# One core's decayed attention: value products dealt over two heads of every four, five probability slots, PSUM banks three and three, and the program's loops written out

## Chip, core and metric

The kernel is one program on 1 core of a Trainium2 chip. It takes the reference's inputs and gives its output. The metric is the device time in microseconds (us), the median of several runs; the profile is one more execution, taken by the hardware profiler.

## What is computed

`x` is 8 sequences of 512 tokens of 128 channels, in float32. Four blocks follow one another, each on a layer norm of `x` and each added to `x`: a Mamba block with a cumulative branch (stage "m" of the kernel), two transformer layers with windowed attention and a gated feed-forward (stage "t0"), the decayed attention below (stage "a"), and the same two layers again (stage "t1").

```python
q, k, v = qkv[0], qkv[1], qkv[2]                 # 16 heads of 8 channels, from x @ Wqkv.T + b
scores = einsum('bhsd,bhtd->bhst', q, k) / sqrt(8)
decay = exp(-abs(distance_decay[0]) * abs(s - t))
attn = softmax(scores * decay, axis=-1)          # 512 x 512 per head
out = einsum('bhst,bhtd->bhsd', attn, v)
return out.transpose(...).reshape(b, s, e) @ out_w.T + out_b
```

## The kernel before

Every engine has an instruction list of its own, written by hand, and the lists meet only through semaphores. Each stage walks over its B = 8 sequences; the first and the last one or two are written out, and the ones between are a hardware loop (`Fori`), whose body is in the program once and ends in a branch back. All semaphore targets in a loop body are computed from the loop's register. Between stages all engines wait for each other (`meet`).

Stage "a", for sequence q and head h (16 heads), with query tiles or key chunks 0 to 3:

- TensorE `score` (line 1165): one bf16 product of 72 by 128 with 72 by 512 makes the scores of one query tile t; it goes to `bank[t % 2]`, so two PSUM banks alternate. It waits until VectorE has read the score two before it.
- VectorE `scale_scores` (1319): times the decay, and the row maximum, PSUM to the tile `S[h % 4, t]`.
- GpSimd `subtract_max` (1403): maximum minus score, in place.
- TensorE `turn` (1174): four 128 by 128 transposes bring key chunk c of the head into `bank[2 + c]`: four banks, one for each chunk. The chunk-0 turn waits for the head's four `subtract_max`, and each turn for the exponentials of four turns earlier.
- ScalarE `exps` (1276): the exponential of the turned chunk, from its bank to `AT[h % 4, c]`.
- TensorE `weigh` (1185): once four heads are done, their probabilities times their values (and ones, for the sums) for key chunk c, four products side by side in `bank[6]`. With c = 0 it waits for the division of the group before.
- ScalarE `copy_oT` (1280), TensorE `untranspose` (1192), VectorE `divide` (1331, 1334): the result of four heads is copied, turned back and divided by its sums.

TensorE's list sets the order. A sequence is 64 steps u = 4h + c. In each it issues `SCORES[u % 16]` scores (they run LEAD = 6 scores ahead of the turns), then perhaps a `weigh`, then the turn. Before the change the four `weigh` of a group stand in the four steps of the next group's first head, with two scores in front of each; the next twelve steps have eight scores. `untranspose` stands behind the second head, and `divide` in VectorE's list behind the first score (t = 0) of a group.

Once for each sequence there are further steps: projections of the next sequence on TensorE (1149, 1154), their copies on ScalarE (1268, 1269), the values' copy `take_values` on VectorE (1325), the split of queries and keys into three bf16 parts on GpSimd (`split`, 1390, 1394, 1397, behind heads 6 and 8), the bias and norm work for the next stage, the output projection of the sequence before, and SyncE's transfers of the parts through DRAM.

Of the kernel before, what the change touches and what calls it, by code (L numbers as in the profile page):

```python
# [21 lines left out]
P = 128  # L22
# [31 lines left out]
LEAD = 6  # L54
SCORES = (2, 2, 2, 2, 1, 1, 1, 0, 1, 1, 0, 1, 0, 1, 0, 1)

# [81 lines left out]
def hybrid_block(nc, a, out):  # L138
# [3 lines left out]
    with ctx:  # L142
# [78 lines left out]
        amax = mem.take(4, TPS)  # L221
        AT = mem.take(4, TPS, L)
        aoT = mem.take(L)
# [99 lines left out]
        MAMBA_LOADS, FOLD_LOADS = 11, 3  # L323
        COMBOS = 2 * PARTS
        HALF = HA // 2 * L
        FIRST = 2 * TPS
# [15 lines left out]
        def hold(eng):  # L342
# [7 lines left out]
                   (hidden_ready, 2), (down_added, 1),  # L350
                   (scaled_done, 2), (aexp_done, TPS), (at_done, 16), (ao_ready, 1), (av_out, TPS),
                   (xt_ready, 1), (lt_ready, 1), (mm_ready, 1), (mixed, 1), (gT_ready, 1), (fuse_added, 1))
# [110 lines left out]
        def transformer_sp(sp, call, meets):  # L463
# [10 lines left out]
            for l in range(DEPTH):  # L474
                q0 = l * B + call * SEQS
                if l:
# [4 lines left out]
                    load_ff(sp, l)  # L481
                with sp.Fori(0, B - 1) as s:
# [25 lines left out]
        def transformer_pe(pe, call, meets):  # L508
# [151 lines left out]
            for l in range(DEPTH):  # L660
# [18 lines left out]
                attention_sequence(q0, False, True)  # L679
                with pe.Fori(1, B - 1) as s:  # L680
                    attention_sequence(q0 + s, True, True)
# [8 lines left out]
                ff_round(q0 + 1, 1, False, True)  # L690
                with pe.Fori(2, B - 2, 2) as s:
                    ff_round(q0 + s, 0, False, True)
                    ff_round(q0 + s + 1, 1, False, True)
# [7 lines left out]
        def transformer_act(act, call, meets):  # L701
# [75 lines left out]
            for l in range(DEPTH):  # L777
# [7 lines left out]
                attention_sequence(q0, False, True)  # L785
                with act.Fori(1, B - 1) as s:
                    attention_sequence(q0 + s, True, True)
# [6 lines left out]
                ff_affine(q0, 0)  # L794
                with act.Fori(0, B - 2, 2) as s:
                    ff_round(q0 + s, 0, True)
                    ff_round(q0 + s + 1, 1, True)
# [33 lines left out]
        def transformer_dve(dve, call, meets):  # L831
# [125 lines left out]
            for l in range(DEPTH):  # L957
# [10 lines left out]
                if l == 0:  # L968
                    with dve.Fori(1, B - 2) as s:
                        attention_sequence(s, q0 + s, True, True, True)  # L970
                    attention_sequence(B - 2, q0 + (B - 2), True, True)
                else:
                    with dve.Fori(1, B - 1) as s:
                        attention_sequence(s, q0 + s, True, True)
# [7 lines left out]
                ff_round(1, q0 + 1, 1, False, True, last_layer)  # L982
                with dve.Fori(2, B - 2, 2) as s:
                    ff_round(s, q0 + s, 0, False, True, last_layer)
                    ff_round(s + 1, q0 + s + 1, 1, False, True, last_layer)
# [14 lines left out]
        def transformer_pool(pool, call, meets):  # L1000
# [58 lines left out]
            for l in range(DEPTH):  # L1059
# [6 lines left out]
                if l == 0:  # L1066
                    with pool.Fori(0, B - 2) as s:
                        attention_sequence(s, q0 + s, True, True)
                    attention_sequence(B - 2, q0 + (B - 2), True)
                else:  # L1070
                    with pool.Fori(0, B - 1) as s:
                        attention_sequence(s, q0 + s, True)
# [3 lines left out]
                meet(pool, l * 2 + meets + 1)  # L1076
                with pool.Fori(0, B - 2, 2) as s:
# [21 lines left out]
        def decayed_sp(sp):  # L1099
# [19 lines left out]
            load_ff(sp, 0)  # L1119
            with sp.Fori(0, B - 1) as q:  # L1120

# [11 lines left out]
        def decayed_pe(pe):  # L1133
# [24 lines left out]
            def score(q, k):  # L1158
                if k == 0:
                    pe.wait_ge(combos_in[0], (q + 1) * (16 * COMBOS))  # L1160
                if k == 32:
                    pe.wait_ge(combos_in[1], (q + 1) * (16 * COMBOS))
                h, t = k // TPS, k % TPS
                pe.wait_ge(scaled_done, 64 * q + k + 1)
                nc.tensor.matmul(bank[t % 2][:, :], QC[0:COMBO, h, t * P:(t + 1) * P], KC[0:COMBO, h, :],  # L1165
                                 start=True, stop=True).then_inc(score_done, 1)

            def turn(q, h, c):
# [4 lines left out]
                for t in range(TPS):  # L1173
                    last = nc.tensor.transpose(bank[2 + c][:, t * P:(t + 1) * P], S[:, h % 4, t, c * P:(c + 1) * P], ident)  # L1174
                last.then_inc(at_done, 1)

            def weigh(q, g, c):

                pe.wait_ge(aexp_done, 64 * q + 16 * g + c + 17)
                if c == 0:  # L1180
# [3 lines left out]
                for i in range(4):  # L1184
                    last = nc.tensor.matmul(bank[6][32 * i:32 * i + 2 * DA, :], AV[:, c, 4 * g + i, :], AT[:, i, c, :],
                                            start=(c == 0), stop=(c == TPS - 1), skip_group_check=True)
# [25 lines left out]
            def sequence(q, before, more):  # L1212
                k = LEAD
                for u in range(HA * TPS):
                    h, c = u // TPS, u % TPS
                    for _ in range(SCORES[u % 16]):
# [4 lines left out]
                        k += 1  # L1221
                    if h % 4 == 0:
                        if h:
                            weigh(q, h // 4 - 1, c)
                        elif before:
                            weigh(q - 1, 3, c)
                    turn(q, h, c)
                    if c < TPS - 1:
                        continue
                    if h == 1:  # L1230
                        if before:
                            untranspose(q - 1, 3)
                        project_v(q)
                    elif h % 4 == 1:
                        if before and h == 5:
                            out_transpose(q - 1, True, more)
                        untranspose(q, h // 4 - 1)
# [13 lines left out]
            sequence(0, False, True)  # L1251
            with pe.Fori(1, B - 1) as q:
                sequence(q, True, True)
# [7 lines left out]
        def decayed_act(act):  # L1261
# [9 lines left out]
            def exps(q, h):  # L1271
                for c in range(TPS):
                    act.wait_ge(at_done, 64 * q + 4 * h + c + 17)
                    if h % 4 == 0:
                        act.wait_ge(av_out, 16 * q + h + c + 1)
                    nc.scalar.activation(AT[:, h % 4, c, :], bank[2 + c][:, :], ACT.Exp, scale=-1.0).then_inc(aexp_done, 1)  # L1276

# [8 lines left out]
            def sequence(q, before, more):  # L1286
                for h in range(HA):
                    exps(q, h)
                    if h == 0 and before:
                        copy_oT(q - 1, 3)  # L1290
                    elif h % 4 == 0 and h:
                        copy_oT(q, h // 4 - 1)
# [12 lines left out]
            sequence(0, False, True)  # L1305
            with act.Fori(1, B - 1) as q:
                sequence(q, True, True)
# [4 lines left out]
        def decayed_dve(dve):  # L1312
            def scale_scores(q, h, t):
                if t == 0:
# [3 lines left out]
                off = (TPS - 1 - t) * P  # L1318
                nc.vector.tensor_tensor_reduce(out=S[:, h % 4, t, :], in0=bank[t % 2][:, :], in1=decay[:, off:off + L],  # L1319
                                               scale=1.0, scalar=-3.0e38, op0=ALU.mult, op1=ALU.max,  # L1320
# [21 lines left out]
            def sequence(q, before, more, norm_more=False, norm_next=False):  # L1342
                for h in range(HA):
                    for t in range(TPS):
                        scale_scores(q, h, t)
                        if t == 0 and h < 8 and h % 4 == 0 and before:
# [18 lines left out]
            sequence(0, False, True, True)  # L1365
            with dve.Fori(1, B - 2) as q:
                sequence(q, True, True, True)
# [6 lines left out]
        def decayed_pool(pool):  # L1374
# [46 lines left out]
            for t in range(2):  # L1421
                for step in range(3):
                    split(0, t, step)
            with pool.Fori(0, B - 2) as q:
                sequence(q, True, True)
# [99 lines left out]
        def mamba_pe(pe):  # L1525
# [124 lines left out]
            sequence(0, 0, False, True, True)  # L1650
            with pe.Fori(0, (B - 4) // 2) as s:
                sequence(2 * s + 1, 1, True, True, True)
# [10 lines left out]
        def mamba_act(act):  # L1663
# [76 lines left out]
            sequence(0, 0, False, True, True)  # L1740
            with act.Fori(0, (B - 4) // 2) as s:
                sequence(2 * s + 1, 1, True, True, True)
# [8 lines left out]
        def mamba_dve(dve):  # L1751
# [118 lines left out]
            sequence(0, 0, False, True, True, True)  # L1870
            with dve.Fori(0, (B - 4) // 2) as s:
                sequence(2 * s + 1, 1, True, True, True, True)
# [9 lines left out]
        def mamba_pool(pool):  # L1882
# [100 lines left out]
            sequence(0, 0, False, True, True, True)  # L1983
            with pool.Fori(0, (B - 4) // 2) as s:
                sequence(2 * s + 1, 1, True, True, True, True)
# [110 lines left out]
```

## Time and profile before

| | us |
|---|---|
| median of 3 runs (2385.03 to 2386.71) | 2386.45 |
| the profiled execution's own time | 2385.01 |
| its span, first to last instruction | 2383.2 |
| stage "m" and start | 0 to 330 |
| stage "t0" | 330 to 1053 |
| stage "a" (first score to last addition) | 1071.9 to 1635.1 |
| stage "t1" | 1635.1 to 2383.2 |

A timeline row gives an instruction's start, its duration, and in brackets how long its engine had been idle and who ended that. TensorE's ends are modelled: a matmul's duration reaches past the start of the next one, so the true cost of a step on TensorE is the distance between starts. An idle time in brackets is therefore shorter than the delay of the start. Times are us from the start of the span.

### The profile page before, as it was taken

To read this page: it belongs to the slowest core of one execution; us is meant where nothing else is said; L and a number is where in the kernel's file an instruction comes from. 1 tells how busy PE (TensorE), PEld (TensorE's weight loads), DVE (VectorE), ACT (ScalarE), POOL (GpSimd) and SP (SyncE) were. 2 spreads that over 40 slices of the span, in tenths; PEclk is the share of its full clock that TensorE was granted. 3 is DMA by queue.
4 is the path that set the end of the run, shared out by engine and by line. 5 is a ranking of instruction groups with operands and counts; after the bars stand their busy time and mean duration, and the time that the engine had idled before them with its cause. 6 is when DMAs were issued, how large, how long until landed. Compare 5 with 4: busy or idle time off the path is not lost. (4 is left out here: it accounts for less than half of the span.)

```text
span 2383.2 us, 60302 instructions
## 1 busy us (share of the span) xinstructions
PE 2184.3 (92%) x19744; PEld 1490.5 (63%) x19760; DVE 1627.2 (68%) x3905; ACT 1489.7 (63%) x4130; POOL 1679.1 (70%) x1712
## 2 busy tenths in 40 slices
PE   6998789998989999859999999998999978999979
PEld 4766557776557777535655656564777755677755
DVE  5777578886557777537666667675878745777755
ACT  3556368887358887325655556554888843888853
POOL 5777788886168888228777777766889822888842
PEclk8999899999999999889999999998999999999999
DMA  4000011111111111112111111101111112111101
GB/s 111 1 0 1 6 27 34 40 37 30 48 36 36 36 34 33 27 58 58 54 42 34 52 53 37 49 21 25 28 34 40 43 23 51 36 34 36 39 21 50
DMA packets 121250, 86.69 MB, mean 36 GB/s; under 512 B 85560, under 2 KB 102160, under 8 KB 118800
## 3 DMA queue, kind: packets, MB, share of 16 engines
q1 hardware_dynamic: 119248, 82.70, 14.3%
q10 hardware_dynamic: 1856, 2.23, 0.3%
q8 instruction: 69, 1.13, 0.2%
q14 instruction: 77, 0.63, 0.1%
HBM read 30.38 MB, written 8.39 MB: 16 GB/s over the span
## 5 line engine op out<-in xcount | busy, mean ns | idle before, releaser
L1319 DVE CUSTOM_DVE_ANT_0 store<-bank,store 128x512 f32<-128x512 f32 x512 | 340.1, 689 | 170.2 <-PE bank L1165 108.6
L1403 POOL TENSOR_SCALAR store<-store 128x512 f32<-128x512 f32 x512 | 349.7, 694 | 149.5 <-DVE store L1319 147.4
L1276 ACT ACTIVATE store<-bank 128x512 f32<-128x512 f32 x512 | 287.1, 603 | 251.2 <-PE bank L1174 247.7
L730 ACT ACTIVATE store<-bank,store 128x128 f32<-128x128 f32 x1024 | 364.2, 378 | 68.5 <-DVE store L860 68.4
L1010 POOL TENSOR_TENSOR store<-store 128x16 f32<-128x16 f32 x128 | 372.5, 2910 | 26.6 <-DVE store L856 26.6
L1004 POOL TENSOR_TENSOR store<-store 128x512 f32<-128x512 f32 x256 | 321.0, 1275 | 85.0 <-DVE store L847 83.7
L1174 PEld LDWEIGHTS bank<-store 128*128 128x128 f32 x2048 | 241.4, 142 | 130.4 <-ACT store L1276 74.1
L1174 PE MATMUL bank<-store 128*128 128x128 f32 x2048 | 298.3, 278 | 0.0
L519 PE MATMUL bank<-store 128*128 128x512 f32 x512 | 270.1, 615 | 7.1 <-DVE store L835 6.6
L1019 POOL TENSOR_TENSOR store<-store 128x512 f32<-128x512 f32 x256 | 261.5, 1043 | 17.4 <-POOL store L1010 11.4
L860 DVE TENSOR_REDUCE store<-bank 128x4 f32<-128x512 f32 x256 | 165.0, 686 | 130.4 <-PE bank L553 130.4
L736 ACT ACTIVATE store<-bank 128x512 f32<-128x512 f32 x256 | 157.8, 616 | 114.0 <-PE bank L566 114.0
L730 ACT ACTIVATION_READ_ACCUMULATOR store<-bank,store 128x1 f32 x1024 | 222.1, 217 | 0.0
L1165 PE MATMUL bank<-store 72*128 72x512 bf16 x512 | 183.2, 389 | 39.5 <-DMA store<-parts 22.0
L638 PE MATMUL bank<-store 128*128 128x512 f32 (+1 forms) x384 | 189.4, 630 | 27.8 <-DVE store L933 22.8
L533 PEld LDWEIGHTS bank<-store 128*128 128x128 f32 x1024 | 116.3, 141 | 129.1 <-POOL store L1019 103.2
L533 PE MATMUL bank<-store 128*128 128x128 f32 x1024 | 154.8, 281 | 35.1 <-POOL store L1019 33.1
L842 DVE TENSOR_TENSOR store<-bank,store 128x512 f32<-128x512 f32 x256 | 174.5, 682 | 12.9 <-issue 6.2
L847 DVE TENSOR_TENSOR store<-bank,store 128x512 f32<-128x512 f32 x256 | 174.4, 681 | 0.0
L592 PEld LDWEIGHTS bank<-store 128*128 128x128 f32 x1024 | 133.5, 192 | 63.8 <-ACT store L741 38.7
L762 ACT ACTIVATE store<-bank,store 128x512 f32<-128x512 f32 (+1 forms) x96 | 65.9, 686 | 170.7 <-PE bank L638 168.4
L566 PEld LDWEIGHTS bank<-store 128*128 128x128 f32 x1024 | 120.8, 141 | 75.9 <-issue 68.1
(199 smaller groups left out, 4457.3 us busy)
## 6 DMA issues: line engine op xcount, KB each, us to landing
store<-store SPq DMA_DIRECT2D x256, 128.0 KB, 2.3
store<-parts SPq DMA_DIRECT2D x96, 192.0 KB
parts<-store SPq DMA_DIRECT2D x16, 384.0 KB, 3.6
store<-store SPq DMA_DIRECT2D x128, 32.0 KB
store<-store SPq DMA_DIRECT2D x128, 31.8 KB
store<-store SPq DMA_DIRECT2D x32, 127.0 KB
store<-in_L_ffn_wqkv_dram SPq DMA_DIRECT2D x4, 768.0 KB, 4.6
out_dram<-store SPq DMA_DIRECT2D x8, 256.0 KB, 2.5
```

Source lines behind the costliest of these rows:

```text
L519: nc.tensor.matmul(bank[i][:, :], hT[:, j * P:(j + 1) * P], wqkv[:, i * INNER:(i + 1) * INNER], start=True, stop=True).then_inc(qk_done, 1)
L533: last = nc.tensor.transpose(bank[5 + i][:, b * P:(b + 1) * P], roped[:, i, b * P:(b + 1) * P], ident)
L638: nc.tensor.matmul(to, w1[:, half * HID + at:half * HID + at + n], fnT[:, odd, :], start=True, stop=True).then_inc(up_done, 1)
L730: last = nc.scalar.activation(prob[:, e, b, :], bank[3 + e][:, b * P:(b + 1) * P], ACT.Exp, bias=nmax[:, e, b:b + 1], accum_out=psums[:, h ...
L1004: nc.gpsimd.tensor_tensor(straight[:, at, :], straight[:, at, :], turned[:, at, :], ALU.add).then_inc(add_done, 1)
L1010: nc.gpsimd.tensor_tensor(flat, flat, minus_half[:, 0:2 * H], ALU.pow).then_inc(norm_done, 1)
L1019: nc.gpsimd.tensor_tensor(roped[:, i, :].rearrange("p (h d) -> p h d", d=DH), straight[:, at, :].rearrange("p (h d) -> p h d", d=DH), bc(n ...
L1165: nc.tensor.matmul(bank[t % 2][:, :], QC[0:COMBO, h, t * P:(t + 1) * P], KC[0:COMBO, h, :], start=True, stop=True).then_inc(score_done, 1)
L1174: last = nc.tensor.transpose(bank[2 + c][:, t * P:(t + 1) * P], S[:, h % 4, t, c * P:(c + 1) * P], ident)
L1276: nc.scalar.activation(AT[:, h % 4, c, :], bank[2 + c][:, :], ACT.Exp, scale=-1.0).then_inc(aexp_done, 1)
L1319: nc.vector.tensor_tensor_reduce(out=S[:, h % 4, t, :], in0=bank[t % 2][:, :], in1=decay[:, off:off + L], scale=1.0, scalar=-3.0e38, op0=A ...
L1403: nc.gpsimd.tensor_scalar(s_, s_, -1.0, amax[:, h % 4, t:t + 1], ALU.mult, ALU.add).then_inc(shifted_done, 1)
```

## The change

Three things in stage "a", and one all over:

1. The order. `weigh` stands in steps 1, 3, 5 and 7 of the next group, so in its first two heads, one in front of every second turn. `SCORES` gives these two heads 5 and 5 scores and the other two 3 and 3. A result slot is now read while the next group's second head is being made, so `AT` has a ring of five head slots in place of four. `copy_oT` moves behind the exponentials of the group's second head, `untranspose` behind its third head, `divide` behind the score t = 2, and `take_values` from head 4, t = 0 to head 3, t = 3.
2. The banks. Scores use three banks in turn and turned chunks three, in place of two and four. The waits follow: a score waits for the reading of the score three before it, a turn for the exponential three before it.
3. `Fori` becomes Python's `for ... in range(...)` in every loop of every engine and stage, so each loop body stands in the program as often as it runs, with constants where registers were.

```diff
-SCORES = (2, 2, 2, 2, 1, 1, 1, 0, 1, 1, 0, 1, 0, 1, 0, 1)
+RING = 5
+SCORES = (1, 2, 0, 2, 1, 1, 1, 2, 1, 0, 1, 1, 1, 0, 1, 1)
-        AT = mem.take(4, TPS, L)
+        AT = mem.take(RING, TPS, L)
+        SCORE_BANKS, TURN_BANKS = 3, 3
-                   (scaled_done, 2), (aexp_done, TPS), (at_done, 16), (ao_ready, 1), (av_out, TPS),
+                   (scaled_done, SCORE_BANKS), (aexp_done, TURN_BANKS), (at_done, 16), (ao_ready, 1), (av_out, TPS),
...
-                nc.tensor.matmul(bank[t % 2][:, :], QC[0:COMBO, h, t * P:(t + 1) * P], KC[0:COMBO, h, :],
+                nc.tensor.matmul(bank[(64 * q + k) % SCORE_BANKS][:, :], QC[0:COMBO, h, t * P:(t + 1) * P], KC[0:COMBO, h, :],
...
-                    last = nc.tensor.transpose(bank[2 + c][:, t * P:(t + 1) * P], S[:, h % 4, t, c * P:(c + 1) * P], ident)
+                    last = nc.tensor.transpose(bank[SCORE_BANKS + (64 * q + 4 * h + c) % TURN_BANKS][:, t * P:(t + 1) * P], S[:, h % 4, t, c * P:(c + 1) * P], ident)
...
-                pe.wait_ge(aexp_done, 64 * q + 16 * g + c + 17)
+                pe.wait_ge(aexp_done, 64 * q + 16 * g + c + 13 + TURN_BANKS)
...
-                    if h % 4 == 0:
-                        if h:
-                            weigh(q, h // 4 - 1, c)
+                    if h % 4 < 2 and c % 2:
+                        part = 2 * (h % 4) + c // 2
+                        if h > 1:
+                            weigh(q, h // 4 - 1, part)
                         elif before:
-                            weigh(q - 1, 3, c)
+                            weigh(q - 1, 3, part)
...
-            with pe.Fori(1, B - 1) as q:
+            for q in range(1, B - 1):
                 sequence(q, True, True)
...
-                    if h % 4 == 0:
-                        act.wait_ge(av_out, 16 * q + h + c + 1)
-                    nc.scalar.activation(AT[:, h % 4, c, :], bank[2 + c][:, :], ACT.Exp, scale=-1.0).then_inc(aexp_done, 1)
+                    if h % 4 == 1:
+                        act.wait_ge(av_out, 16 * q + h + c)
+                    nc.scalar.activation(AT[:, (16 * q + h) % RING, c, :], bank[SCORE_BANKS + (64 * q + 4 * h + c) % TURN_BANKS][:, :], ACT.Exp, scale=-1.0).then_inc(aexp_done, 1)
...
-                        if t == 0 and h >= 8 and h % 4 == 0:
+                        if t == 2 and h >= 8 and h % 4 == 0:
                             divide(q, h // 4 - 2)
-                        if t == 0 and h == 4:
+                        if t == 3 and h == 3:
                             take_values(q)
...
-                pool.wait_ge(scaled_done, 64 * q + 4 * h + t + 3)
+                pool.wait_ge(scaled_done, 64 * q + 4 * h + t + 1 + SCORE_BANKS)
```

## Rows read from the trace of the kernel before

**Rows 1.** Stage "a": us, busy PE, PEld, DVE, ACT, POOL (count), clock, DMA share.

```profile
1071.90:1635.10 563.20, 543.56 (x3928) 334.22 (x3928) 386.92 (x1200) 322.79 (x587) 413.32 (x583) 0.98 0.16 43
```

**Rows 2.** TensorE's waits from 1084 to 1620: total us, times, longest.

```profile
PE bank L1165 <- DVE store L1319: 16.0, 36, 1.7
```

**Rows 3.** The same view over stage "a" whole.

```profile
PE bank L1165 <- DMA store<-parts: 22.0, 1, 22.0
...
PE bank L1165 <- DVE store L1319: 17.2, 39, 1.7
```

**Rows 4.** TensorE's timeline at the beginning of a group.

```profile
1247.13 0.38 PE L1165 MATMUL bank<-store 72*128 72x512 bf16 x1
1247.80 0.39 PE L1165 MATMUL bank<-store 72*128 72x512 bf16 x1 [0.29 <-DVE store L1319]
1248.12 1.05 PE L1185 MATMUL bank<-store 128*16 128x512 f32 x8
1249.10 0.65 PE L1174 MATMUL bank<-store 128*128 128x128 f32 x4
1249.59 0.60 PE L1165 MATMUL bank<-store 72*128 72x512 bf16 x2
```

**Rows 5.** Timeline around VectorE's branch back at 1273.5.

```profile
1273.37 0.69 DVE L1319 CUSTOM_DVE_ANT_0 store<-bank,store 128x512 f32<-128x512 f32 x1
...
1276.63 0.69 DVE L1319 CUSTOM_DVE_ANT_0 store<-bank,store 128x512 f32<-128x512 f32 x1 [2.56 <-PE bank L1174]
...
1277.39 0.39 PE L1165 MATMUL bank<-store 72*128 72x512 bf16 x1 [1.56 <-DVE store L1319]
```

**Rows 6.** Busy time of two sequences (columns as in 1).

```profile
1282.06:1352.30 70.24, 67.37 (x493) 41.34 (x493) 48.48 (x151) 40.64 (x75) 52.57 (x74) 1.00 0.16 46
1352.30:1424.13 71.83, 68.96 (x492) 42.83 (x492) 48.48 (x151) 40.84 (x75) 52.59 (x74) 0.98 0.16 46
```

**Rows 7.** DMA queues, 1214 to 1556 (all loops), then 340 to 383 (written out).

```profile
q14 instruction: 19, 0.16, 0.2%
...
q8 instruction: 4, 0.07, 0.7%
```

**Rows 8.** VectorE in a transformer loop: behind a taken branch, and leaving the loop.

```profile
789.78 0.29 DVE L835 COPY store<-bank 128x128 f32<-128x128 f32 x1 [0.98 <-PE bank L513]
...
926.20 0.29 DVE L835 COPY store<-bank 128x128 f32<-128x128 f32 x1 [0.98 <-PE bank L513]
```

**Rows 9.** TensorE's waits in that loop, 702 to 925.

```profile
PE bank L533 <- POOL store L1019: 2.3, 13, 0.2
```

**Rows 10.** Timeline: from a score to GpSimd, from a turn to ScalarE.

```profile
1200.05 0.60 PE L1165 MATMUL bank<-store 72*128 72x512 bf16 x2
...
1200.62 0.69 DVE L1319 CUSTOM_DVE_ANT_0 store<-bank,store 128x512 f32<-128x512 f32 x1 [0.69 <-PE bank L1165]
...
...
1201.53 1.36 POOL L1403 TENSOR_SCALAR store<-store 128x512 f32<-128x512 f32 x2 [0.64 <-DVE store L1319]
...
1219.33 0.66 PE L1174 MATMUL bank<-store 128*128 128x128 f32 x4
...
1220.10 0.60 ACT L1276 ACTIVATE store<-bank 128x512 f32<-128x512 f32 x1 [1.41 <-PE bank L1174]
...
1220.59 0.59 ACT L1280 ACTIVATE store<-bank 128x512 f32<-128x512 f32 x1
```

**Rows 11.** GpSimd's groups in one sequence: count, busy us, mean ns.

```profile
L1403 POOL TENSOR_SCALAR store<-store 128x512 f32<-128x512 f32 x64 | 43.7, 693 | 16.8 <-DVE store L1319 16.6
L1390 POOL TENSOR_TENSOR store<-store 128x512 f32<-128x512 f32 x2 | 2.3, 1163 | 0.0
...
L1394 POOL CAST store<-store 128x512 bf16<-128x512 f32 x2 | 1.2, 610 | 0.3 <-POOL store L1390 0.3
```

**Rows 12.** VectorE's timeline: its extra work behind head 9.

```profile
1248.99 0.69 DVE L1340 TENSOR_TENSOR store<-bank,store 128x512 f32 x1
...
1251.04 0.69 DVE L1319 CUSTOM_DVE_ANT_0 store<-bank,store 128x512 f32<-128x512 f32 x1
```

More of the change, by code:

```diff
@@ L481, in transformer_sp @@
                     load_ff(sp, l)
-                with sp.Fori(0, B - 1) as s:
+                for s in range(0, B - 1):
                     if l == 0:
@@ L679, in transformer_pe @@
                 attention_sequence(q0, False, True)
-                with pe.Fori(1, B - 1) as s:
+                for s in range(1, B - 1):
                     attention_sequence(q0 + s, True, True)
@@ L690, in transformer_pe @@
                 ff_round(q0 + 1, 1, False, True)
-                with pe.Fori(2, B - 2, 2) as s:
+                for s in range(2, B - 2, 2):
                     ff_round(q0 + s, 0, False, True)
@@ L785, in transformer_act @@
                 attention_sequence(q0, False, True)
-                with act.Fori(1, B - 1) as s:
+                for s in range(1, B - 1):
                     attention_sequence(q0 + s, True, True)
@@ L794, in transformer_act @@
                 ff_affine(q0, 0)
-                with act.Fori(0, B - 2, 2) as s:
+                for s in range(0, B - 2, 2):
                     ff_round(q0 + s, 0, True)
@@ L968, in transformer_dve @@
                 if l == 0:
-                    with dve.Fori(1, B - 2) as s:
+                    for s in range(1, B - 2):
                         attention_sequence(s, q0 + s, True, True, True)
@@ L972, in transformer_dve @@
                 else:
-                    with dve.Fori(1, B - 1) as s:
+                    for s in range(1, B - 1):
                         attention_sequence(s, q0 + s, True, True)
@@ L982, in transformer_dve @@
                 ff_round(1, q0 + 1, 1, False, True, last_layer)
-                with dve.Fori(2, B - 2, 2) as s:
+                for s in range(2, B - 2, 2):
                     ff_round(s, q0 + s, 0, False, True, last_layer)
@@ L1066, in transformer_pool @@
                 if l == 0:
-                    with pool.Fori(0, B - 2) as s:
+                    for s in range(0, B - 2):
                         attention_sequence(s, q0 + s, True, True)
@@ L1070, in transformer_pool @@
                 else:
-                    with pool.Fori(0, B - 1) as s:
+                    for s in range(0, B - 1):
                         attention_sequence(s, q0 + s, True)
@@ L1076, in transformer_pool @@
                 meet(pool, l * 2 + meets + 1)
-                with pool.Fori(0, B - 2, 2) as s:
+                for s in range(0, B - 2, 2):
                     for odd in range(2):
@@ L1119, in decayed_sp @@
             load_ff(sp, 0)
-            with sp.Fori(0, B - 1) as q:
+            for q in range(0, B - 1):
                 for half in range(2):
@@ L1184, in weigh @@
                 for i in range(4):
-                    last = nc.tensor.matmul(bank[6][32 * i:32 * i + 2 * DA, :], AV[:, c, 4 * g + i, :], AT[:, i, c, :],
+                    last = nc.tensor.matmul(bank[6][32 * i:32 * i + 2 * DA, :], AV[:, c, 4 * g + i, :], AT[:, (16 * q + 4 * g + i) % RING, c, :],
                                             start=(c == 0), stop=(c == TPS - 1), skip_group_check=True)
@@ L1230, in sequence @@
                     if h == 1:
-                        if before:
-                            untranspose(q - 1, 3)
                         project_v(q)
-                    elif h % 4 == 1:
-                        if before and h == 5:
-                            out_transpose(q - 1, True, more)
+                    if h == 5 and before:
+                        out_transpose(q - 1, True, more)
+                    if h == 2 and before:
+                        untranspose(q - 1, 3)
+                    elif h % 4 == 2 and h > 2:
                         untranspose(q, h // 4 - 1)
@@ L1288, in sequence @@
                     exps(q, h)
-                    if h == 0 and before:
+                    if h == 1 and before:
                         copy_oT(q - 1, 3)
-                    elif h % 4 == 0 and h:
+                    elif h % 4 == 1 and h > 1:
                         copy_oT(q, h // 4 - 1)
@@ L1305, in decayed_act @@
             sequence(0, False, True)
-            with act.Fori(1, B - 1) as q:
+            for q in range(1, B - 1):
                 sequence(q, True, True)
@@ L1318, in scale_scores @@
                 off = (TPS - 1 - t) * P
-                nc.vector.tensor_tensor_reduce(out=S[:, h % 4, t, :], in0=bank[t % 2][:, :], in1=decay[:, off:off + L],
+                nc.vector.tensor_tensor_reduce(out=S[:, h % 4, t, :], in0=bank[(64 * q + 4 * h + t) % SCORE_BANKS][:, :], in1=decay[:, off:off + L],
                                                scale=1.0, scalar=-3.0e38, op0=ALU.mult, op1=ALU.max,
@@ L1345, in sequence @@
                         scale_scores(q, h, t)
-                        if t == 0 and h < 8 and h % 4 == 0 and before:
+                        if t == 2 and h < 8 and h % 4 == 0 and before:
                             divide(q - 1, 2 + h // 4)
-                        if t == 0 and h >= 8 and h % 4 == 0:
+                        if t == 2 and h >= 8 and h % 4 == 0:
                             divide(q, h // 4 - 2)
-                        if t == 0 and h == 4:
+                        if t == 3 and h == 3:
                             take_values(q)
@@ L1365, in decayed_dve @@
             sequence(0, False, True, True)
-            with dve.Fori(1, B - 2) as q:
+            for q in range(1, B - 2):
                 sequence(q, True, True, True)
@@ L1423, in decayed_pool @@
                     split(0, t, step)
-            with pool.Fori(0, B - 2) as q:
+            for q in range(0, B - 2):
                 sequence(q, True, True)
@@ L1650, in mamba_pe @@
             sequence(0, 0, False, True, True)
-            with pe.Fori(0, (B - 4) // 2) as s:
+            for s in range(0, (B - 4) // 2):
                 sequence(2 * s + 1, 1, True, True, True)
@@ L1740, in mamba_act @@
             sequence(0, 0, False, True, True)
-            with act.Fori(0, (B - 4) // 2) as s:
+            for s in range(0, (B - 4) // 2):
                 sequence(2 * s + 1, 1, True, True, True)
@@ L1870, in mamba_dve @@
             sequence(0, 0, False, True, True, True)
-            with dve.Fori(0, (B - 4) // 2) as s:
+            for s in range(0, (B - 4) // 2):
                 sequence(2 * s + 1, 1, True, True, True, True)
@@ L1983, in mamba_pool @@
             sequence(0, 0, False, True, True, True)
-            with pool.Fori(0, (B - 4) // 2) as s:
+            for s in range(0, (B - 4) // 2):
                 sequence(2 * s + 1, 1, True, True, True, True)
```

## The prediction

> **What bounds the kernel now.** I read the busy time by stage first. In stage "a" TensorE is busy for 543.6 of 563.2 us, and the others for 413 and less [rows 1]: TensorE's list sets the time, and only a later start of one of its steps costs anything. So I went to its waits. Once the stage runs, TensorE waits for one thing only: `score` for VectorE's reading of the bank, 36 times, 16.0 us [rows 2]. The timeline shows the true price. Two scores follow each other at 0.22 us (0.60 for two, against 0.38 for one), but the second at the beginning of a group comes 0.67 after the first: 0.45 late for an idle time of 0.29 [rows 4], since the modelled end hides 0.16. With that, 36 waits cost 16.0 + 36 x 0.16 = 21.8 us.
>
> They are of three kinds. 24 are the 0.29 of [rows 4]: three scores stand close together (last step of a group, then two) and two banks can't hold them; 24 x 0.45 = 10.8 us. Four stand where VectorE branches back in its loop (sequences 1 to 4): its next score comes 3.3 us after the last, 2.56 of it idle, and TensorE idles 1.56 [rows 5]. The view ascribes VectorE's idle time to a turn that had ended long before; what is there is the branch. The four idle times are 1.60, 1.56, 1.75 and 1.75, so 6.7 + 0.6 = 7.3 us. Eight smaller ones (3.6 us) lie where VectorE has other work in front of the scores, 2.05 us behind head 9 [rows 12]. In one sequence the idle time at the branch was followed by a stretch with half the clock: 71.83 us at a mean clock of 0.98, where its neighbour took 70.24 at 1.00 [rows 6]. These 1.6 us go with the wait.
>
> **The order and the banks.** The work on TensorE is the same: as many scores (0.22), turns (0.44) and `weigh` (start to start 0.98, plus 0.10 in front and 0.05 in the turn behind [rows 4]). Each `weigh` has a score in front and a turn behind, before and after. A group is 16 x 0.22 + 16 x 0.44 + 4 x 1.13 + 0.44 (`untranspose`) = 15.5 us; four and the sequence's extras (4.4) make 66.4, what a sequence takes without its waits (70.24 less 3 x 0.45, 0.59 and 1.91 [rows 6] is 66.4).
>
> Scores with three banks: a bank is free about 1.36 us after its score's start (0.57 to VectorE's start, 0.69 its work [rows 10], an estimated 0.1 for the signal). In the new order the closest four scores are those of the last step (0), step 0 (0.66) and step 1 (1.32 and 1.54): the fourth needs the first, at 1.36. No wait. After head 9 VectorE is busy 2.05 us [rows 12]; the scores behind it (steps 3, 3 and 4) stand 2.2 to 4.2 us after those of step 1, and the third bank takes them. In the last sequence VectorE normalizes eight tiles there, and I leave 0.4 us. So 21.8 falls to 0.4. At the stage's start three more waits cost 1.2 us (17.2 against 16.0 [rows 2, 3]); the third bank takes these too, while the 22.0 us for the first transfer stay [rows 3].
>
> Turns with three banks: a turn needs the exponential of three turns before. From a turn's start to its exponential's is 0.77, the exponential 0.60 [rows 10], the signal 0.1: 1.47. The closest four turns (steps 8 to 11) span 1.76: 0.44, then 0.66 twice; step 9 has no score. But there `copy_oT` now stands between, with 0.49 before the next exponential can start [rows 10]: exponential 7 at 0.77 after its turn, the copy at 1.26, exponential 8 at 1.75, ended at 2.35, and turn 11 is due at 2.42. It is late by 0 to 0.1; in group 1, where ScalarE also copies the transposed output, by 0.15. I take 1.2 us for 32 groups, with 0 and 3 as bounds.
>
> GpSimd: the turn of head 0 of a group needs `subtract_max` of its fourth score, which is now issued in step 12, 2.64 us before (0.66 + 0.44 + 0.66 + 0.66 for steps 12 to 15, 0.22 for the score of step 0; in the old order 4.2 us). The chain is 0.57 to VectorE, 0.91 from there to GpSimd [rows 10], 0.68 its work, 0.1: 2.26. `divide` now stands in front of that score in VectorE's list, waits for `untranspose` (done about 0.2 after the score's start) and takes 0.54, so VectorE starts 0.2 later: 2.4 to 2.45 of 2.64. That holds, by 0.2 us, and it is the tightest place. Behind head 8 (group 2) `split` stands behind that same score in GpSimd's list: 1.16 + 0.61 + 1.16 [rows 11] and 0.2 of waits is 3.1 us, then four `subtract_max` at 0.68. They end 2.33 + 3.1 + 2.7 = 8.15 us after the score; the second head's turn is due at 7.77 (2.42 to the group's end, 5.13 for steps 0 to 3 with two `weigh`, 0.22) and comes about 0.4 to 0.5 late. In the old order it was due at about 11. Seven sequences have it: 3.2 us (bounds 0 and 6). The `split` behind head 6 has 2 us to spare. Nothing that waits for these turns is late elsewhere; SyncE's transfers, which wait for `split` and for scores, are as early as before within 1 us.
>
> `take_values` moved before head 4 waits for the values' projection, at most 1.3 us, and VectorE has that: 16 scores at 0.69 are 11 us of a group of 16.6. The fifth slot makes the exponentials of the second head wait only for `weigh` steps issued before them.
>
> **The loops.** Written out, VectorE's list has no branch in stage "a", so the 7.3 and 1.6 go. In other stages I expect nothing: behind a taken branch VectorE idles 0.98 us, and 0.98 where it leaves the loop [rows 8]; TensorE's waits there are 13 of at most 0.2, for GpSimd [rows 9]. What straight code could cost is fetching. While all engines loop in stage "a", 19 instruction packets (8 KB) still come on one queue; in written-out code four of 16 KB come on the other in 43 us [rows 7]. The Trainium skill ("Runtime: NRT & Kernel Launch", Instruction fetch mechanics) says that blocks are fetched ahead in sequence, and that a taken branch to a block no longer held has to wait for it; packets within the loops fit that. At the pace of those four, 220 come in the whole span. But the written-out sequences show on TensorE no wait but those for banks, so I cost fetching at nothing; at 0.03 us each it would be 7 us, and the upper end holds that.
>
> **Sum.** Gone: 21.8 - 0.4 + 1.6 + 1.2 = 24.2. New: 3.2 + 1.2 = 4.4. Net 19.8 on the profiled execution's 2385.0 (span 2383.2), so 2365.2; the median of the runs is 1.4 above that execution: 2366.5 us.
>
> **Rivals.**
> - *Half of it* (0.13). The banks' waits go, but VectorE still stalls on its code, now at block ends, or the bounds of the new waits hold (6 + 3): 8 to 10 us less gain, 2376. For it: packets come in straight code too [rows 7]. Against: no wait of such a size in the written-out sequences.
> - *Slower, GpSimd's chain* (0.05). If the chain from the fourth score to the turn is longer than 2.64, each of 32 groups pays. From 2.64 + 19.8 / 32 = 3.26 us on the change is no gain. If VectorE had to wait for `untranspose` and divide in full before it (1.0 more than 2.26 and some queueing, 3.6 us), it would cost 31 us: 2397. For it: `divide` stands right in front of the score. Against: `untranspose` is issued a step before that score.
> - *No change* (0.03). A turn bank fewer costs in each group what a score bank more gives: 0.6 us at each `copy_oT`. That needs an exponential 0.6 later than [rows 10] has it.
> - *Gains in every loop* (0.04). VectorE has 23 other taken branches; at 1.8 us each TensorE would gain 41 more, 2325. By the skill's rule on taken branches (same section) each far target costs a fetch. [rows 8, 9] speak against it: the same idle time with and without the branch.
>
> **The numbers.** My forecast has 0.75, with a range of its own from 2360 to 2372. About 0.2% (4.8 us) is what a measurement of this kernel can tell from no change. Low end: all of 21.8 + 1.6 + 1.2 = 24.6 gone, no new waits, 3 us from lighter loops, 2359. High end: the half case with some more, 2380. Faster: 0.75 + 0.13 + 0.04 = 0.92; same 0.03; slower 0.05.
>
> **What the profile after would show.** No wait of `score` for VectorE but one or two in the last sequence; VectorE's gap at a new sequence under 1 us; sequences of 66.4 to 67.5 us; a turn waiting for `subtract_max` about 0.4 us once a sequence behind head 8; granted clock 1.00 until the end of the stage; transformer stages within 1 us of before. Wrong if turns wait at every group's start, or for exponentials at every `copy_oT`.

## The result and the profile after

The changed kernel takes 2357.51 us (median of 4 runs, 2354.70 to 2359.53), the kernel before 2386.58 beside it: a ratio of 0.9877, with a 95% interval of 0.9860 to 0.9894. That is 29.1 us less; I had forecast 19.9 less (2366.5), with 2359 as the low end. The direction was right, and the gain larger than the range allowed. Two executions of this study, one of 2823 us of the kernel before and one of 3641 us in experiment 6, ran at a low granted clock (0.74 and 0.56) and are left out of the ratios.

The profiled execution took 2359.53 us, with a span of 2357.7. Between the points where all engines meet, taken where TensorE comes to them in both traces:

| us | before | after | difference |
|---|---|---|---|
| stage "m" | 291.4 | 295.8 | +4.4 |
| stage "t0" | 750.5 | 744.9 | -5.6 |
| stage "a", with its start | 591.2 | 568.5 | -22.7 |
| stage "t1" | 750.1 | 748.4 | -1.7 |

Stage "a" first. Busy time of a sequence, and of the stage (columns as in [rows 1]):

```profile
1215.53:1282.14 66.61, 66.42 (x494) 41.63 (x493) 48.41 (x150) 41.34 (x74) 52.51 (x75) 1.00 0.17 48
...
1070.40:1609.60 539.20, 534.22 (x3923) 333.87 (x3924) 386.35 (x1199) 327.76 (x587) 413.17 (x583) 0.99 0.17 46
```

TensorE's waits from 1084 to 1590 (the answer to [rows 2]):

```profile
PE bank L1176 <- POOL store L1406: 1.7, 7, 0.5
PE bank L1167 <- DVE store L1322: 0.2, 1, 0.2
```

Every sequence from the second to the last but one takes 66.6 us (they took 67.6 to 71.8). The 36 waits for score banks have become one. The one new wait is the forecast one: seven times, once a sequence, a turn waits for GpSimd. TensorE's timeline there:

```profile
1245.72 0.38 PE L1167 MATMUL bank<-store 72*128 72x512 bf16 x1
1246.30 0.66 PE L1176 MATMUL bank<-store 128*128 128x128 f32 x4 [0.19 <-POOL store L1406]
```

The turn should follow the score by 0.22 us and follows by 0.58: 0.36 late.

Now what I had not forecast. GpSimd in a transformer loop, the power (L1010, then L1012) and the scaling behind it (L1019, then L1021). The kernel before:

```profile
762.77 2.91 POOL L1010 TENSOR_TENSOR store<-store 128x16 f32<-128x16 f32 x1 [0.21 <-DVE store L856]
765.90 2.04 POOL L1019 TENSOR_TENSOR store<-store 128x512 f32<-128x512 f32 x2 [0.22 <-POOL store L1010]
```

The changed kernel at the same place:

```profile
764.51 2.91 POOL L1012 TENSOR_TENSOR store<-store 128x16 f32<-128x16 f32 x1 [0.21 <-DVE store L858]
767.50 2.05 POOL L1021 TENSOR_TENSOR store<-store 128x512 f32<-128x512 f32 x2
```

The gap was 0.22 us (52 of 128 times, two in each of the 26 loop passes, and 0.08 the other 76 times), and is 0.08 every time. TensorE's transposes (533) wait for this scaling. In the loop of [rows 9] their waits fall from 2.3 us to 0.3:

```profile
PE bank L535 <- POOL store L1021: 0.3, 1, 0.3
```

Instruction packets from 1214 to 1556, all written out now:

```profile
q8 instruction: 21, 0.34, 0.4%
q14 instruction: 18, 0.15, 0.1%
```

Code now comes as it runs, 21 packets of 16 KB on the queue that had none there before, and TensorE shows no wait for it.

The +4.4 us in stage "m" is no added work. By VectorE's list the changed kernel is level with the kernel before (0.3 us) until 46 us, 3.9 us behind at 57, and 4.4 to 5.1 behind from 82 us to the end of the stage. The granted clock stands in these rows; the kernel before, then the changed one:

```profile
32.00:50.00 18.00, 11.62 (x31) 7.42 (x33) 9.91 (x18) 9.36 (x16) 11.34 (x15) 0.53 0.00 0
50.00:62.00 12.00, 11.95 (x73) 9.50 (x73) 8.31 (x18) 5.45 (x14) 9.20 (x14) 1.00 0.01 1
```

```profile
33.00:58.00 25.00, 18.42 (x61) 12.36 (x62) 11.61 (x22) 10.96 (x17) 14.06 (x17) 0.59 0.00 1
```

The half clock at the start ended at 49.6 us in the one and at 57.4 in the other. Over all profiles of this study stage "m" took 289.4 to 302.2 us, whatever the kernel. That may be a good part of why executions of the kernel before spread from 2382 to 2394 us; only profiled executions show their stages, so it isn't shown. For small effects I read stage lengths and the period of a sequence in stage "a", which repeats to 0.05 us between profiles of one kernel. Stage lengths repeat less well: the two profiles of the changed kernel have 1493.3 and 1495.4 us for the two transformer stages together.

### The profile page after: what moved, and what is told of

Same layout as the page of the kernel before. It is cut to its first block and busy times, and to the rows that moved or that the text cites. A ratio compares the mean times of both kernels' runs of the same rounds, so it can differ in the third digit from the quotient of the medians.

```text
span 2357.7 us, 54563 instructions
## 1 busy us (share of the span) xinstructions
PE 2171.4 (92%) x19760; PEld 1488.6 (63%) x19760; DVE 1618.5 (69%) x3905; ACT 1484.6 (63%) x4122; POOL 1679.7 (71%) x1712
## 5 line engine op out<-in xcount | busy, mean ns | idle before, releaser
L1012 POOL TENSOR_TENSOR store<-store 128x16 f32<-128x16 f32 x128 | 372.8, 2912 | 26.1 <-DVE store L858 26.1
L1176 PE MATMUL bank<-store 128*128 128x128 f32 x2048 | 300.8, 277 | 2.6 <-POOL store L1406 2.2
L1021 POOL TENSOR_TENSOR store<-store 128x512 f32<-128x512 f32 x256 | 261.8, 1044 | 10.0
L535 PE MATMUL bank<-store 128*128 128x128 f32 x1024 | 159.3, 284 | 29.6 <-POOL store L1021 27.8
```

The source lines that it names most:

```text
L535: last = nc.tensor.transpose(bank[5 + i][:, b * P:(b + 1) * P], roped[:, i, b * P:(b + 1) * P], ident)
L1012: nc.gpsimd.tensor_tensor(flat, flat, minus_half[:, 0:2 * H], ALU.pow).then_inc(norm_done, 1)
L1021: nc.gpsimd.tensor_tensor(roped[:, i, :].rearrange("p (h d) -> p h d", d=DH), straight[:, at, :].rearrange("p (h d) -> p h d", d=DH), bc(n ...
L1176: last = nc.tensor.transpose(bank[SCORE_BANKS + (64 * q + 4 * h + c) % TURN_BANKS][:, t * P:(t + 1) * P], S[:, h % 4, t, c * P:(c + 1) * P ...
```

## Experiments

Twelve runs of ten new kernels (two runs are repeats), each timed beside the kernel before on the same chip. Ratios are against it, with 95% intervals.

**1. All loops written out, old order and banks**

```diff
-            with dve.Fori(1, B - 2) as q:
+            for q in range(1, B - 2):
```

and so for all 20 loops.

> The kernel before with every loop written out, its old order and its old banks. Main theory: writing out gives 7.3 us (four branches back in VectorE's list of stage a), mostly also 1.6 us (the half clock that followed one of them), and about 7 us in the transformer stages; the waits of the scores for two banks stay. Sequences of stage a at about 68.2 us, time 2370 to 2372. Rival (the written-out loops only help together with the new order, because VectorE still stalls on its code): 2378 or more, and VectorE's gap of 2.6 us at a new sequence stays.

Measured: 2369.97 us, 0.9925 (0.9904 to 0.9947), 17.1 less. Stage "a" falls by 8.7 us (591.2 to 582.5), its sequences to 68.3 us, the transformer stages by 7.6. As the main theory has it.

**2. The changed stage "a", loops kept in the other stages**

```diff
-            for s in range(1, B - 1):
+            with pe.Fori(1, B - 1) as s:
```

and so for all loops outside stage "a".

> The changed kernel with the loops of all stages but a put back. Main theory: the 22.6 us of stage a stay whole, and the 7 us of the transformer stages are lost: 2364 to 2365, which is what my forecast was a forecast of; GpSimd's gap between the power and the scaling is 0.22 us again for 52 tiles. Rival (the transformer stages' gain was chance of the clock, or came from stage a): 2357 to 2358, as the changed kernel.

Measured: 2366.65 us, 0.9907 (0.9884 to 0.9931). Stage "a" 568.2 us; the transformer stages take 1500.1 together, as before (1500.6), where the changed kernel takes 1493.3. The gaps of 0.22 are back, 52 of them. What I had forecast, 2366.5, lies within the noise of this kernel's time (its executions took 2362 to 2373): most of my error is what the loops outside stage "a" were worth.

**3. Only the transformer stages' loops written out**

> The kernel before with the loops of the two transformer stages written out on all engines, nothing else. Main theory: 7 us less, 2379 to 2380; the gaps of 0.22 us between GpSimd's power and scaling become 0.08 (52 of them, 7.3 us). Rival (nothing to be had in those loops, as I forecast): 2386.

Measured: 2370.11 us, 0.9926 (0.9906 to 0.9946): 16.9 less, more than twice what the theory had. In its profile the transformer stages take 1490.9 us, 9.7 less, and stage "a", untouched, 581.2: 10.0 less. VectorE's stall at the branch back is gone, with the branch still there (at 1268.0 us). VectorE's timeline at that place (compare [rows 5]):

```profile
1267.90 0.69 DVE L1319 CUSTOM_DVE_ANT_0 store<-bank,store 128x512 f32<-128x512 f32 x1
...
1268.67 0.69 DVE L1319 CUSTOM_DVE_ANT_0 store<-bank,store 128x512 f32<-128x512 f32 x1
```

In the kernel before, 16 instruction packets (its queue q14) come between 1214 and 1480 us; in the same stretch of this kernel the queue has no row, while the loops run. The row of that queue in the kernel before, then the only row of this one:

```profile
q14 instruction: 16, 0.13, 0.2%
```

```profile
q1 hardware_dynamic: 4626, 12.07, 16.2%
```

So "a branch back stalls" was not the whole of it. The body of that loop is the same; what is different is all that lies in front of it in VectorE's list. Experiment 9 tests this. Experiments 4 and 6 leave VectorE's list as it was, and there all four stalls stay (2.56 to 2.68 us), with their packets.

**4. Only GpSimd's loops of the transformer stages written out**

> The kernel before with only GpSimd's loops of the transformer stages written out; TensorE, VectorE, ScalarE and SyncE keep theirs. Main theory (the target of a wait, computed in GpSimd's list between two instructions of the path that TensorE waits for): nearly all of the gain of writing out all engines' loops, 6 to 7 us, 2380. Rival (the branches and register work of TensorE's or VectorE's lists): under 2 us, 2385.

Measured: 2378.40 us, 0.9964 (0.9948 to 0.9979), 8.6 less. The transformer stages take 1493.8 us, 6.8 less; the changed kernel has 7.3 less. GpSimd alone gives all that the loops' passes give: by the starts of GpSimd's power, a pass of the first layer's attention loop took 34.50 us and takes 34.37, one of the second layer's took 34.10 and takes 33.83, the same to 0.02 as in the changed kernel. The gap is 0.08 in all 128 places, as here (the power runs from 762.84 to 765.75 us):

```profile
765.83 2.05 POOL L1019 TENSOR_TENSOR store<-store 128x512 f32<-128x512 f32 x2
```

**5. Only VectorE's loop in stage "a" written out**

```diff
-            with dve.Fori(1, B - 2) as q:
+            for q in range(1, B - 2):
```

> The kernel before with one loop written out: VectorE's in stage a. Main theory: VectorE's four gaps of 2.56 to 2.75 us at a new sequence go, and with them 7.3 us and the 1.6 us of half clock where they brought it: 2377 to 2379. Rival (the gap belongs to the wait for the turn or for the division behind it, not to the branch): 2386, with the gap there.

Measured: 2375.99 us, 0.9950 (0.9937 to 0.9962), 10.2 less. The gaps are gone and the sequences take 68.1 us. The price of the stall and its half clock, 8.9 us, was sized nearly rightly; the median is just below the 2377 to 2379 that I expected. The profiled execution was the slowest of its six, 2385.56 us, with 302.2 us in stage "m" (half clock again); its stage "a" takes 580.1, 11.1 less.

The half clock is another matter. In the kernel before it followed one of the four stalls (the sequence of 71.8 us). In experiments 4 and 6, with the same four stalls, it followed none: their sequences with a stall take 70.0 to 70.2 us, against 68.3 for the next. So the stall costs 1.8 to 1.9 us each time, and the 1.6 us of half clock came in one of the three profiles that have the stalls.

**6. The waits in GpSimd's `normalize` turned round, loops kept**

```diff
-                if i == 0:
-                    pool.wait_ge(norm_done, 4 * q + j + 1)
                 pool.wait_ge(add_done, n2 + i + 1)
                 pool.wait_ge(qkT_done, n2 + i + 1)
+                if i == 0:
+                    pool.wait_ge(norm_done, 4 * q + j + 1)
```

> The kernel before, all loops kept; in GpSimd's normalize the same three waits in another order, the one for the power last, so that the targets of the other two are computed while the power runs. Main theory: the gap between power and scaling falls from 0.22 to about 0.08 us and the time by 5 to 7 us, 2380 to 2381, as with the loops written out. Rival (the gap is the hardware's way of starting an instruction in a loop): no change of the gap, 2386.

Measured: 2385.79 us, 0.9997 (0.9987 to 1.0007). A miss. The gap is neither 0.22 nor 0.08, but 0.17, in all 128 places (21.7 us in sum, the second view):

```profile
765.69 2.91 POOL L1010 TENSOR_TENSOR store<-store 128x16 f32<-128x16 f32 x1 [0.21 <-DVE store L856]
768.77 2.04 POOL L1019 TENSOR_TENSOR store<-store 128x512 f32<-128x512 f32 x2 [0.17 <-POOL store L1010]
```

```profile
L1019 POOL TENSOR_TENSOR store<-store 128x512 f32<-128x512 f32 x256 | 261.6, 1043 | 21.7 <-POOL store L1010 21.7
```

The trace also has the steps of GpSimd's sequencer, the part that reads the list, computes targets and waits. They tell the places apart:

| gap, us | where | which instruction waits for the power | computations of targets behind the power |
|---|---|---|---|
| 0.08 | before, 76 places; changed kernel and experiment 4, all 128 | the scaling itself | none |
| 0.22 | before, 52 places | one ahead of the scaling, with a computation | two, and another wait |
| 0.17 | experiment 6, 52 places | a wait ahead of the scaling | one |
| 0.17 | experiment 6, 76 places | a wait ahead of the scaling | none |

So register work alone isn't what costs. In 76 places of experiment 6 no target is computed behind the power, and the gap is still 0.17. Every place with 0.08 has the wait for the power in the scaling itself; in all others it stands in an instruction of its own ahead of the scaling. In the kernel before, a computed target put it there; here the order of the waits did. That is read from the traces and not tested by itself. A pass of the first layer's loop takes 34.55 us (34.50 before), one of the second's 34.02 (34.10): a loss and a gain that cancel.

**7. The new order with two banks for scores and four for turns**

```diff
-        SCORE_BANKS, TURN_BANKS = 3, 3
+        SCORE_BANKS, TURN_BANKS = 2, 4
```

> The changed kernel with two banks for scores and four for turned chunks. Main theory: with two banks the scores of steps 0 and 1, and of 6 and 7, stand too close (0.66 us, and 1.36 us until a bank is free): about 0.5 us late twice in a group, 32 groups, 25 to 32 us: 2382 to 2390. Rival (the order does the work and the third bank is idle reserve): 2358 to 2362.

Measured: 2388.88 us, 1.0009 (1.0000 to 1.0017), 31 us above the changed kernel; a sequence takes 71.0 us. TensorE's waits from 1084 to 1590, and its timeline at the first of two late scores in a group (the second, at 1253.67, waits 0.53):

```profile
PE bank L1167 <- DVE store L1322: 20.3, 68, 0.6
```

```profile
1249.51 0.39 PE L1167 MATMUL bank<-store 72*128 72x512 bf16 x1
1250.53 0.39 PE L1167 MATMUL bank<-store 72*128 72x512 bf16 x1 [0.63 <-DVE store L1322]
```

The new order puts scores closer than two banks can take, twice in a group.

**8. The old order with three and three banks, loops written out**

```diff
-RING = 5
-SCORES = (1, 2, 0, 2, 1, 1, 1, 2, 1, 0, 1, 1, 1, 0, 1, 1)
+RING = 4
+SCORES = (2, 2, 2, 2, 1, 1, 1, 0, 1, 1, 0, 1, 0, 1, 0, 1)
...
-                    if h % 4 < 2 and c % 2:
+                    if h % 4 == 0:
```

with `copy_oT`, `untranspose`, `divide` and `take_values` in their old places.

> The changed kernel with three and three banks and all loops written out, but the old order: four weigh in the first head, scores 8 there and 8 behind, four probability slots, copy, untranspose and divide in their old places. Main theory: the third bank takes the three close scores in the old order too, and GpSimd has more time there, so nothing is lost and the 0.36 us behind head 8 (seven times) may be won: 2355 to 2358. Rival (dealing the weigh over two heads is what frees TensorE, and three turn banks don't do for the old order): 2364 or more.

Measured: 2354.88 us, 0.9863 (0.9847 to 0.9879). Its sequences take 66.6 us, as those of the changed kernel; only one takes 67.0.

**9. The kernel before, VectorE's list shifted by 64 instructions**

```diff
+        spare = mem.take(64)
...
+            for i in range(64):
+                nc.vector.memset(spare[:, i:i + 1], 0.0)
             nc.vector.memset(bank[6][:, :], 0.0)
             sequence(0, False, True, True)
```

> The kernel before with all its loops, and 64 one-element memsets on VectorE at the start of stage a, where it idles 27 us for the first scores; they shift all that follows in its list. Theory, formed after the run with only the transformer loops written out: whether a branch back stalls depends on where the loop's body lies on the blocks in which instructions are fetched. Then the four gaps of 2.6 us and the packets fetched in each turn of the loop go, with the loop still there: 2376 to 2379. Rival (the branch itself stalls, and the other run lost its stall for another reason): 2386, with the gaps.

Measured: 2376.44 us, 0.9965 (0.9952 to 0.9979): 64 more instructions and 9.0 us less. The branch is there, no gap over 1.6 us is left among the scores' reductions, the sequences take 68.3 us, and from 1214 to 1480 no instruction packet comes. VectorE's timeline behind the branch:

```profile
1271.13 0.69 DVE L1320 CUSTOM_DVE_ANT_0 store<-bank,store 128x512 f32<-128x512 f32 x1
...
1271.93 0.69 DVE L1320 CUSTOM_DVE_ANT_0 store<-bank,store 128x512 f32<-128x512 f32 x1
```

**10. The changed kernel, the second `split` behind head 9**

```diff
-                    if more and h in (6, 8):
+                    if more and h in (6, 9):
                         for step in range(3):
-                            split(q + 1, h // 2 - 3, step)
+                            split(q + 1, h // 9, step)
```

> The changed kernel with the second split of a sequence behind head 9 in place of head 8 in GpSimd's list. Theory: the turn that waits 0.36 us for subtract_max once in each of seven sequences no longer waits, 2.5 us less than the changed kernel. Rival (the wait moves to the norm work behind head 10, or SyncE's transfers come too late): same or slower than the changed kernel.

Measured: 2354.41 us, 0.9866 (0.9849 to 0.9882). TensorE's wait for GpSimd is gone and the sequences take 66.3 us, 0.3 less (one of the six measured takes 66.6). In the profile that is 1.9 us of stage "a" (567.6 in experiment 11 to 565.7); in the medians 0.35, less than their noise.

**11 and 12. The changed kernel, and experiment 8's, again beside it**

> The changed kernel once more, as the measure for the others of this call: 2357 to 2359.

> The kernel with the new banks, all loops written out and the old order once more, beside the changed kernel on one chip. Theory: the order is worth nothing, and the old one is 1 to 3 us faster. Rival (its lead of 2.6 us was between two chips): equal or slower.

Measured: 2354.76 (0.9869, 0.9854 to 0.9884) and 2355.21 us (0.9870, 0.9855 to 0.9885). Equal, and the first below the 2357 to 2359 that I expected of it. In experiment 12's profile TensorE waits for a score bank twice, 1.5 us; in experiment 11's for GpSimd as above. The lead of experiment 8 was between two chips. No version is measurably faster than the changed kernel.

## Why the prediction was wrong

**In stage "a" the mechanism was right.** The waits for banks, 21.8 us, are gone but one of 0.2. The new waits are seven of 0.36 (I had 0.45), 2.5 us of the 3.2 that I took, and one of 0.3 for an exponential in the whole stage (I took 1.2). The dense sequence of 66.4 us is there: 66.6 less 0.36 is 66.25. In sum 22.7 less where I had 19.8: the new waits are 1.6 us less than I took, and the dense sequence is 0.15 us shorter, 1.2 for eight. One term was partly luck: I had the 1.6 us of half clock go with the stall, and experiments 4 and 6 have the stall without it. It was there in the one profile that I had read.

**The step that failed is "In other stages I expect nothing".** The loops outside stage "a" are worth 7.3 us by the two profiles (1500.6 to 1493.3), and experiment 2, which keeps them, comes out at my 2366.5 within its noise. Over all profiles with GpSimd's loops of these stages written out they take 1490.9 to 1495.4 us, and 1497.9 to 1501.4 with the loops as they were. Experiment 4 puts the gain in GpSimd's list. The 52 gaps are 0.14 us shorter, which would be 7.3 us if TensorE felt each of them whole; by the passes it doesn't. The first layer's passes are 0.13 us shorter, the second's 0.27, and 12 and 14 passes make 5.3 us. That 7.3 came out twice is chance, and the rest, about 2 us, is within what these stages differ between two profiles of one kernel.

I had looked for the price of a branch, at VectorE [rows 8], and found none there, rightly. The price was in the loop's body: with a computed target the wait for the power stood ahead of the scaling, on the way that TensorE waits for. The sign of it stood in the profile of before, in GpSimd's group, and I didn't follow it:

```profile
L1019 POOL TENSOR_TENSOR store<-store 128x512 f32<-128x512 f32 x256 | 261.5, 1043 | 17.4 <-POOL store L1010 11.4
```

In the changed kernel that row ends in 10.0 us idle, with no releaser. And I let the 13 waits of [rows 9] pass as small, 0.2 us at most, although they sum to 2.3 us in one loop of four; its seven passes gave 1.9.

**The cause of VectorE's stall was half right.** That it came from the branch back and its size held (experiments 1 and 5), its half clock not always. But it isn't the branch alone: 64 harmless instructions in front take it away with the loop in place (experiment 9), and so does written-out code of other stages (experiment 3), while with VectorE's list untouched it stays (experiments 4 and 6). What stands in front of the loop in VectorE's own list decides, and with it whether packets come in each pass. The Trainium skill ("Runtime: NRT & Kernel Launch", Instruction fetch mechanics) fits that: it has a branch wait only if its target is no longer in the window of two blocks. I had quoted the rule and not asked which loops it spares, nor that a shift could spare this one. It was the rival "Gains in every loop" that held a grain of truth, for another reason than it gave.

**What the parts are worth.** Loops written out: 17 us (experiment 1), about 9 in stage "a" and 5 to 8 in the others. Three banks for scores: 13 to 15 more (experiment 8 against 1). The new order: nothing (experiments 11 and 12), and with two banks it costs 19 to 20 (experiment 7 against 1). My working for the third bank never needed the new order, since it showed three close scores; I didn't ask what the order was for.

**The rest.** The median lies 2 us under the profiled execution, and the second measurement is 2354.8. The low end of my range had 3 us for "lighter loops"; that was the term to be 5 to 7.

Three things stay open. Why a wait ahead of the scaling costs 0.09 to 0.14 us more than one in it is read from the sequencer's steps and not tested by itself. That the stall depends on how the loop's body lies on the fetched blocks is the likely reading of experiments 3 and 9, but only one shift, of 64 instructions, was tried. Whether another place of the list would bring the stall into one of the other loops wasn't tried either.

## What to carry to other kernels

A hardware loop can cost in two places that the branch itself doesn't show. One is the waits in its body with computed targets: where one of them stood ahead of an instruction of a chain that another engine waits for, the step took up to 0.14 us longer here. The other is fetching, if the body lies badly. Before turning waits round by hand, read from the sequencer's steps which instruction carries the wait that comes last: here turning them round moved it out of the scaling in 76 places and gained nothing. And an idle time times its count is only a bound: here 52 times 0.14 us made 5.3 us, and the length of a loop pass told it. Before such a stall is explained, shift the list by some dozens of instructions and see whether it stays. When two steps of a change feed on one wait, run each with the other's old form: here the bank did the work of both.

## What the runs showed of the hardware that I had not expected

A loop of VectorE of some 300 traced instructions stalls by 2.6 to 2.75 us at every branch back, or not at all, depending on 64 instructions in front of it; with the stall come 5 packets of 8 KB in a pass, without it none. Straight code costs nothing that shows: the changed kernel has 159 and 108 instruction packets in place of 69 and 77, and a sequence of experiment 1, all written out, takes 68.31 us, as one of experiment 3 with the loops kept and no stall. On GpSimd an instruction that itself waits for the one before it follows by 0.08 us; with that wait in an instruction of its own ahead of it, by 0.17 to 0.22. Of the first 110 us of the program, half clock took 13.7 to 27.3 us in the profiles of this study (20.5 in the kernel before, 23.9 and 20.5 in two profiles of the changed one).
